# Products of the heads' weights in three 16-bit passes, split by GpSimd

## The reference

```python
q_c = rmsnorm(hidden_states @ w_qa, g_qa)                       # 384 wide
q = (q_c @ w_qb).reshape(b, s, NH, QK)                          # 32 heads of 128 + 64
k_c = rmsnorm((hidden_states @ w_kva)[..., :128], g_kva)        # 128 wide
kst = (k_c @ w_kvb).reshape(b, s, NH, ND + VD)                  # keys and values of a head
scores = einsum('bhqd,bhkd->bhqk', query, key_s) * scaling      # with rotary parts
attn = softmax(scores)
out = einsum('bhqk,bhkd->bhqd', attn, v).reshape(b, s, NH * VD)
return out @ w_o
```

## Time and profile before

| what | before |
|---|---|
| runs (median, lowest to highest) | 2041.67 us, 2041.35 to 2043.67 |
| the profiled execution: its time, its span | 2044.69 us, 2042.9 us |
| mean granted clock of TensorE, of full speed | 0.969 |
| PE busy | 1892.5 us (93%) |
| DVE busy | 1321.2 us (65%) |
| ACT busy | 773.2 us (38%) |
| POOL busy | 308.4 us (15%) |

### The profile page before, as it was taken

How to read it: one execution, slowest core, us unless ns; L and a number is a source line. 1 busy time by engine, 2 the same in 40 slices (tenths; PEclk the granted TensorE clock), 3 DMA queues, 4 the chain that set the end, 5 groups by cost and what they waited for, 6 DMA issues and landing times. The chain is left out here.

```text
span 2042.9 us, 32412 instructions
## 1 busy us (share of the span) xinstructions
PE 1892.5 (93%) x11538; PEld 1029.6 (50%) x11538; DVE 1321.2 (65%) x2742; ACT 773.2 (38%) x2020; POOL 308.4 (15%) x596
## 2 busy tenths in 40 slices
PE   4898898559999999999999999999999999859999
PEld 2344444335555555555555555555555555425554
DVE  4678777436666666666666666666666666555554
ACT  3454554233333334433333433333343333332221
POOL 2376675300000000000000000000000000033332
PEclk9899999679999999999999999999999999979999
DMA  5244342332222322232222222223222222243332
GB/s 143 52 86 96 81 95 65 76 91 51 58 58 59 76 56 53 58 76 59 58 58 55 73 58 58 58 58 75 55 55 58 40 39 39 39 138 80 80 82 73
DMA packets 305609, 138.87 MB, mean 68 GB/s; under 512 B 295088, under 2 KB 295344, under 8 KB 303408
## 3 DMA queue, kind: packets, MB, share of 16 engines
q1 hardware_dynamic: 301136, 108.35, 24.8%
q10 hardware_dynamic: 4320, 28.51, 4.0%
HBM read 56.07 MB, written 8.39 MB: 32 GB/s over the span
## 5 line engine op out<-in xcount | busy, mean ns | idle before, releaser
L1031 PE MATMUL out_ps<-m_h,ot_h 128*128 128x512 f16 x1024 | 389.4, 380 | 1.7 <-DVE ot_l L835 1.7
L1032 PE MATMUL out_ps<-m_l,ot_h 128*128 128x512 f16 x1024 | 389.0, 380 | 0.0
L1033 PE MATMUL out_ps<-m_h,ot_l 128*128 128x512 f16 x1024 | 388.9, 380 | 0.0
L756 ACT ACTIVATE qp_h<-qp_ps 128x512 f16<-128x512 f32 x126 | 75.3, 597 | 492.6 <-PE qp_ps L966 492.6
L812 ACT ACTIVATE prob<-s_ps,nmx 128x128 f32<-128x128 f32 x512 | 181.3, 366 | 207.3 <-DVE nmx L905 207.3
L885 DVE SCALAR_TENSOR_TENSOR resid<-out_ps,resid 128x512 f32<-128x512 f32 x256 | 176.1, 688 | 97.1 <-PE out_ps L1033 97.1
L835 DVE SCALAR_TENSOR_TENSOR qp_l<-qp_ps,qp_h 128x512 f16<-128x512 f32 x126 | 87.2, 692 | 234.5 <-ACT qp_h L756 234.5
L1221 POOL MEMSET fpower<- 128x1 f32 x1 | 0.1, 99 | 1392.4 <-POOLq L674 1392.4
L966 PE MATMUL qp_ps<-lat,wp_h 128*128 128x512 f16 x756 | 205.6, 381 | 0.0
L1033 PEld LDWEIGHTS out_ps<-m_h,ot_l 128*128 128x128 f16 x1024 | 100.4, 98 | 121.6 <-issue 1.4
L1031 PEld LDWEIGHTS out_ps<-m_h,ot_h 128*128 128x128 f16 x1024 | 100.5, 98 | 110.5 <-DVE ot_l L835 2.7
(11 more groups left out here) (217 smaller groups left out, 3861.3 us busy)
## 6 DMA issues: line engine op xcount, KB each, us to landing
wide<-heads_in ACTq DMA_DIRECT2D x30, 928.0 KB, 4.7
wide<-x_in SPq DMA_DIRECT2D x30, 512.0 KB, 6.5
tower_out<-result SPq DMA_DIRECT2D x16, 512.0 KB, 2.6
stage<-wb_in SPq DMA_DIRECT2D x8, 512.0 KB, 8.3
resid<-wqk_in SPq DMA_DIRECT2D x1, 2304.0 KB, 11.6
zt<-z SPq DMA_TRANSPOSE x128, 2.4
turned<-halves SPq DMA_TRANSPOSE x128, 3.0
wide<-heads_in SPq DMA_DIRECT2D x2, 928.0 KB, 4.6
```

Source lines behind the costliest of these rows:

```text
L756: act.activation(out, src, ACT.Copy, scale=scale).then_inc(done, 1)
L1031: pe.matmul(out_ps[hf][:, :], ot_h[:, h, :], m_h[:, at], start=h == 0, stop=False)
L1032: pe.matmul(out_ps[hf][:, :], ot_h[:, h, :], m_l[:, at], start=False, stop=False)
L1033: last = pe.matmul(out_ps[hf][:, :], ot_l[:, h, :], m_h[:, at], start=False, stop=h == HEADS - 1)
```

## The change

The products of heads 4 to 31 no longer multiply 32-bit operands. GpSimd takes each head's raw weights in three pieces of 640, 512 and 512 columns (the first holds queries, keys and values), multiplies a piece by 2^8 in place, copies it to a 16-bit high half, and subtracts that from the scaled piece into a 16-bit low half. The halves lie in `wide1`, which is thus no raw buffer any more. PE waits for a piece's low half and sums three 16-bit passes. The scales of the evictions take out 2^16 (`un`). The raw weights of heads from 4 on all go to `wide0`; the load is now issued in the round in which the head is multiplied, for the head 4 rounds ahead, at the same place of ScalarE's order. Heads 0 to 3 keep the 32-bit products. The core of the diff:

```diff
+RAW_S = 2.0**8
+        split = keep["wide1"][:, :].bitcast(F16)
+        split_h, split_l = split[:, 0:RAW_R], split[:, RAW_R:2 * RAW_R]
+        PIECES = [slice(RAW_Q, RAW_O), slice(RAW_O, RAW_O + CHUNK), slice(RAW_O + CHUNK, RAW_R)]
...
             def prod_high(h, p, sd, k, part, bank, fresh):
-
+                un = 1.0 if fresh else RAW_S ** -2
...
             def body(before, now, after, more):
-                if more and (not now.known or now.t + HEADS + 1 < NH):
-                    act.wait_ge(prod_done, now.t * 3 + 3 * HEADS)
+                if more and before:
                     act.wait_ge(wr_lo, now.t + HEADS)
-                    load(now.t + HEADS + 1, 1 - now.parity)
+                    act.wait_ge(raw_lo, (now.t - 1) * 3 + 3)
+                    load(now.t + HEADS, 0)
...
+        @block.gpsimd
+        def _(pool):
+            for h in range(HEADS, NH):
+                pool.wait_ge(raw_loaded[0], (h - HEADS) * 16 + 48)
+                pool.wait_ge(prod_done, h * 3)
+                if h == HEADS:
+                    pool.wait_ge(wr_lo, HEADS)
+                for n, at in enumerate(PIECES):
+                    done = (h - HEADS) * 3 + n
+                    pool.tensor_scalar(keep["wide0"][:, at], keep["wide0"][:, at], RAW_S, None, ALU.mult
+                                       ).then_inc(raw_scaled, 1)
+                    wait_apart(pool, pool_passed, (raw_scaled, done + 1))
+                    pool.tensor_copy(split_h[:, at], keep["wide0"][:, at]).then_inc(raw_hi, 1)
+                    wait_apart(pool, pool_passed, (raw_hi, done + 1))
+                    pool.tensor_tensor(split_l[:, at], keep["wide0"][:, at], split_h[:, at], ALU.subtract
+                                       ).then_inc(raw_lo, 1)
...
+            def split_products(h, part, bank, free):
+                pe.wait_ge(raw_lo, (h - HEADS) * 3 + (part + 1))
+                pe.wait_ge(prod_lo, free)
+                ways = ((split_h, split_h), (split_h, split_l), (split_l, split_h))
+                if part == 0:
+                    for k in range(QT):
+                        for n, (a, b) in enumerate(ways):
+                            last = pe.matmul(bank[:, k * P:(k + 1) * P], a[:, RAW_Q + k * P:RAW_Q + (k + 1) * P],
+                                             b[:, RAW_K:RAW_K + P], start=n == 0, stop=n == 2)
+                else:
+                    at = RAW_O + (part - 1) * CHUNK
+                    for n, (a, b) in enumerate(ways):
+                        last = pe.matmul(bank[:, :], a[:, RAW_V:RAW_V + P], b[:, at:at + CHUNK],
+                                         start=n == 0, stop=n == 2)
+                last.then_inc(prod_done, 1)
...
                     if more and j:
-                        products(now.t + HEADS, now.parity, j - 1, prod_ps, (now.t + HEADS) * 3 + (j - 1))
+                        split_products(now.t + HEADS, j - 1, prod_ps, (now.t + HEADS) * 3 + (j - 1))
```

More of the change, by code:

```diff
@@ L707, in attention_phase @@
              "av_done o_hi o_lo out_done out_added").split())
+        raw_scaled, raw_hi, raw_lo, pool_passed = (sem(n) for n in ("raw_scaled", "raw_hi", "raw_lo", "apool_passed"))
+        split = keep["wide1"][:, :].bitcast(F16)
+        split_h, split_l = split[:, 0:RAW_R], split[:, RAW_R:2 * RAW_R]
+        PIECES = [slice(RAW_Q, RAW_O), slice(RAW_O, RAW_O + CHUNK), slice(RAW_O + CHUNK, RAW_R)]
         resid = keep["resid"]
@@ L762, in prod_high @@
                     high(wp_h[:, bass.ds(sd, 1), :, bass.ds(k, 1), :].rearrange("p a t k n -> p (a t) (k n)"),
-                         bank[:, 0:QR].rearrange("p (t n) -> p t n", t=QT), WP_S, prod_hi)
+                         bank[:, 0:QR].rearrange("p (t n) -> p t n", t=QT), WP_S * un, prod_hi)
                     if not fresh:
@@ L771, in prod_high @@
                     high(m_h[:, bass.ds((sd * HEADS + k) * D + (part - 1) * CHUNK, CHUNK)], bank[:, :],
-                         M_S, prod_hi)
+                         M_S * un, prod_hi)
             def query_high(r, j, bank=qp_ps):
@@ L823, in body @@
                     if more and j:
-                        prod_high(now.t + HEADS, now.parity, now.side * -1 + 1, now.place, j - 1, prod_ps, False)
+                        prod_high(now.t + HEADS, 0, now.side * -1 + 1, now.place, j - 1, prod_ps, False)
                     act.wait_ge(av_done, s + 1)
@@ L836, in low, with prod_low @@
                                          op1=ALU.subtract).then_inc(done, 1)
-            def prod_low(h, p, sd, k, part, bank):
+            def prod_low(h, p, sd, k, part, bank, un=1.0):
                 dve.wait_ge(prod_hi, h * 3 + part + 1)
@@ L842, in prod_low @@
                     low(wp_l[at].rearrange("p a t k n -> p (a t) (k n)"),
-                        bank[:, 0:QR].rearrange("p (t n) -> p t n", t=QT), WP_S,
+                        bank[:, 0:QR].rearrange("p (t n) -> p t n", t=QT), WP_S * un,
                         wp_h[at].rearrange("p a t k n -> p (a t) (k n)"), prod_lo)
@@ L851, in prod_low @@
                     at = bass.ds((sd * HEADS + k) * D + (part - 1) * CHUNK, CHUNK)
-                    low(m_l[:, at], bank[:, :], M_S, m_h[:, at], prod_lo)
+                    low(m_l[:, at], bank[:, :], M_S * un, m_h[:, at], prod_lo)
             def query_low(r, j, bank=qp_ps):
@@ L926, in body @@
                     if more and j:
-                        prod_low(now.t + HEADS, now.parity, now.side * -1 + 1, now.place, j - 1, prod_ps)
+                        prod_low(now.t + HEADS, 0, now.side * -1 + 1, now.place, j - 1, prod_ps, RAW_S ** -2)
                     dve.wait_ge(o_hi, s + 1)
```

## The result

The changed kernel takes 2051.4 us (median of 6 runs, 2048.69 to 2052.67) against 2042.18 us (6 runs, 2040.88 to 2043.67) for the kernel before: a ratio of 1.0044, with a 95% interval of 1.0033 to 1.0055. It is slower, by 9.2 us. The forecast was no change, 2042.7 us; the time lies inside the range, but beyond the 2045.8 us to which "no change" reached: of the three outcomes it is the slower one, which had 36%.

A forecast was written before the change was run, and what follows sets the result against it. PE was taken to bound slots 1 and 2, the VectorE chain slot 0, PE's wait for the queries' low half slot 3. -10.6 + 6.2 + 5.4 = +1.0 us gave 2042.7 us, range 2031 to 2062.

The forecast's parts named there:

- PE's shorter products: 16-bit matmuls save 0.17 us in slot 1 and 0.21 in slot 2, none in slot 3: 10.6 us over 28 heads.
- slot 0: GpSimd's first instruction delays the probabilities' low half by 0.23 us, without slack: 6.2 us over 27 rounds.
- the edits at nothing: Scales, the load's new place, PE's wait for low halves and round 0's load were together taken as zero.
- I take half of the two-input rate: GpSimd's one-input instructions: 0.96 ns a column plus 0.10 us, so 0.71 us for 640 columns and 0.59 for 512.
- the upper end: One-input GpSimd instructions cost at most the two-input rate, 1.92 ns a column: 1.23 us for 640, 0.98 for 512.
- a quarter of a hit: Slot 1: the ninth GpSimd instruction might delay `nmx`, 0.76 us beyond slack; 0.20 us a round charged, 5.4 us.
- slack of 0.25: Slot 1 falls to about 10.37 us, 0.25 above the 10.12 at which the VectorE chain takes over.
- slower rival: One-input GpSimd instructions cost as much as two-input ones, slots 0 and 1 lose: 2076 us; milder form 2058; 36%.
- The rival's 0.75 us: Slot 0's loss if GpSimd's first instruction runs from 5.06 to 6.29 us, at the two-input rate.
- The prediction's test: If GpSimd's first instruction takes 0.87 us or more, slot 0 alone loses 0.39 us and eats the whole gain.
- a case without a hold: Three two-input VectorE instructions ran 3.93 us without a break beside a two-column GpSimd instruction; by this the cost vanishes.
- faster rival: GpSimd's one-input instructions run at the fill's rate and miss `nmx`: 2035.2 us, or 2031.1 without any hold; 27%.

The follow-up runs named there:

- split once: The changed kernel with GpSimd splitting only head 4; heads 5 to 31 reuse its halves and PE waits for the load: 2027.76 us.
- kernel without scalings: The changed kernel with factor 1 and GpSimd's three multiplications left out, casts and subtractions kept: 2036.99 us.
- paced kernel: The changed kernel with one more wait: each GpSimd piece starts after the probabilities' low half of slots 0, 1 and 2: 2026.04 us.
- scalings at z: The changed kernel, but for heads 5 to 31 GpSimd only scales, each scaling started by z's low half in slots 1 to 3: 2032.91 us.

## Why the prediction was right and wrong

| term, rounds 2 to 27 (us) | forecast | measured |
|---|---|---|
| PE's shorter products | -9.9 | -10.4 (split once) |
| slot 0 | +6.0 | +2.6 |
| slot 1 | +5.2 | +20.0 |
| slots 2 and 3 | 0 | +0.3 |
| rounds 0 and 1 | 0 beyond the products' 0.8 | -1.3 beyond them |

(Measured cost of a slot: 26 times the difference of the slot's mean between the changed kernel and the split once.)

**Right: PE.** The nine small matmuls are 0.056 us apart ((0.67 - 0.22)/8) and the three wide ones take 988.58 - 987.93 = 0.65 us. Slots 1 and 2 fall by 0.16 and 0.21 us once GpSimd is out of the way, slot 3 by nothing. Reading a slot's limits from rounds with and without the product was sound.

**Right: the edits at nothing.** No product waits for GpSimd, and the load's new place costs nothing in the rounds.

**Wrong: GpSimd's one-input durations.** The step that failed is "I take half of the two-input rate", and already the upper end beside it. The cast is near its forecast (0.72 and 0.61 us for 0.71 and 0.59). The scaling takes 1.81 and 1.49 us, more than the subtraction's 1.40 and 1.15, which were a little over the forecast too (1.23 and 0.98). The range from the fill to the two-input rate didn't hold the scaling: reading one operand instead of two is no bound for an operation that the trace doesn't show. The Trainium skill (GPSIMD Engine Reference, Engine selection) has one-input work at about line rate; the cast's rows agree ((716 - 610)/128 = 0.83 ns a column, the rate of the fill in the earlier trace rows), the scaling's don't.

**Wrong because of it: slot 1.** The nine instructions end 16.9 us after slot 0's first score in the round shown (972.81 + 1.42 - 957.35) and 16.5 in most, not 13.50. The prediction had one of them near `nmx` and charged a quarter of a hit. In fact the sixth meets `nmx`, the eighth the normalization and the ninth one of the two low halves: 1.16 us, less the slack of 0.25 that the prediction gave slot 1, is 0.91, and 10.36 + 0.91 is the measured 11.27. The slower rival had a 1.16 too, from `nmx` and the normalization alone; its mechanism is the one that took place, its stretch of instructions another, so that the two sums agree is chance. The kernel without scalings, in which the work ends earlier, has a clean slot 1, and the paced kernel has all its lengths and no loss: long instructions cost here only by reaching into the next chain.

**Wrong the other way: slot 0.** The rival's 0.75 us, and my 0.23, took a GpSimd instruction to hold VectorE as long as it lasts. The scaling holds it for 0.69 us, and it starts earlier than I had it: ends at 962.03 + 2.02 = 964.05, less its own 1.81 is 962.24, 0.15 us before z's recorded end. The low half is 0.07 us late. Where the load landed later the hold is bare to see, in round 4 of the changed kernel:

```profile
622.16 1.81 POOL L846 TENSOR_SCALAR wide<-wide 128x640 f32<-128x640 f32 x1 [31.49 <-DMA wide<-heads_in]
622.18 1.23 DVE L857 SCALAR_TENSOR_TENSOR halves<-prob,halves 128x512 f16<-128x512 f32 x1 [0.36 <-ACT halves L761]
```

622.18 + 1.23 - 0.57 - 622.16 = 0.68 us. The prediction's test, that from 0.87 us for the first instruction on slot 0 alone eats the gain, was thus a wrong one: the instruction takes twice that, and slot 0 loses 2.6 us in all. The Trainium skill (SBUF — State Buffer, Who interferes with whom) holds for a whole instruction: for casts and subtractions these rows agree, for scalings they don't, and by the whole instruction the scalings at z would have given 2085 us, not 2033.

**Misread: the earlier trace rows.** The prediction took these rows for a case without a hold. VectorE had started first there (109.44, GpSimd 109.67), and by its length GpSimd's instruction on two columns was the one that stood: 1.64 us, where the shortest of the 16 of its line (L367) took 0.71. So 2031 us, the faster rival's time without any hold, had no row behind it.

**The direction.** The two errors have opposite signs (slot 0 was charged 3.4 us too much, slot 1 14.8 too little), so that the time came out inside the range is in part luck. The sum of a gain of 10 and a cost of 11 was never firm; the range said so, the 0.20 us charged for slot 1 didn't. Its real question was the phase of nine instructions against a chain, and a schedule from three guessed durations can't answer that. Of the signs named for the slower rival, the first instruction over 0.87 us was there, but `nmx` (0.54) and the normalization (0.97) stayed under 1 us.

**Still open.** Why a scaling takes 1.8 us although it holds VectorE no longer than a cast; the no-scaling kernel's early landings, which I took as they came; and slot 1 of round 0.

## What to carry to other kernels

Before giving work to GpSimd beside a busy VectorE chain, ask where each of its instructions will lie against the chain's two-input SBUF instructions, and tie its start to the last of them, if it can end before the next chain begins: one wait on the probabilities' low half was worth some 24 us here (from 9.2 us over the kernel before to 14.5 under it), with the same work done. An operation that the trace doesn't show has no upper price from its neighbours; let the forecast's range and sign depend on it openly. And where two engines meet within 0.1 us, count both outcomes: the load's landing alone chose between a slot of 10.07 and of 11.3 us.

## What the runs showed of the hardware

A GpSimd instruction held VectorE's low half of the probabilities, which reads two SBUF tiles, for 0.69 us with one operand of 640 columns (0.58 with 512) and for 1.37 with two (1.13); `nmx` and the normalization were held too. Casts (0.72 us) and subtractions (1.40) last hardly longer than they hold; a 32-bit scaling in place lasts 1.81 us, and during its last 1.1 us VectorE ran freely. The hold works both ways: a subtraction that met a VectorE low half took 1.62 us instead of 1.40. VectorE's additions into `resid`, one operand of which lies in PSUM, weren't held: beside the paced kernel's GpSimd work they took 0.69 us, as in the kernel before.
